# A graph layer's row gathers: each held for the one two ahead, and the whole ring filled early

## The reference: what is computed

```python
w_full = jnp.einsum('rb,bdo->rdo', w_comp, weight)      # 16 relations from 8 bases
x_rel = jnp.einsum('nd,rdo->rno', feat, w_full)
msg = x_rel[etypes, src] * norm                         # one message per edge
agg = jax.ops.segment_sum(msg, dst, num_segments=N)     # summed by target node
out = agg + h_bias + feat @ loop_weight                 # relu, added to x
...
gate_logits = x @ gate_w + gate_b                       # top 2 of 16 experts
h = relu(einsum('bsh,ehf->bsef', x, w1) + b1)
expert_out = einsum('bsef,efh->bseh', h, w2) + b2
```

## Time and profile before

| | us |
|---|---|
| median of three runs | 3274.21 |
| lowest and highest | 3268.51, 3275.11 |
| span of the profiled execution | 3302.6 |
| GpSimd busy in it | 1809.3 (55%) |
| tensor engine busy in it (matmul) | 2355.1 (71%) |
| DVE, ACT busy in it | 965.9, 658.4 |
| gathers of the layer (L1060), busy and idle before | 1463.5, 974.7 |

### The profile page before, as it was taken

How to read it: one execution, slowest core, us unless ns; L and a number is a source line. 1 busy time by engine, 2 the same in 40 slices (tenths; PEclk the granted TensorE clock), 3 DMA queues, 4 the chain that set the end, 5 groups by cost and what they waited for, 6 DMA issues and landing times. The chain is left out here.

```text
span 3302.6 us, 40335 instructions
## 1 busy us (share of the span) xinstructions
PE 2355.1 (71%) x11549; PEld 1953.5 (59%) x11550; DVE 965.9 (29%) x2172; ACT 658.4 (20%) x1539; POOL 1809.3 (55%) x2000
## 2 busy tenths in 40 slices
PE   2579898877778766767757565654744547999987
PEld 1467777666667555545545454543533337999986
DVE  6352332332223211222122121211211235333338
ACT  3232322222112211101110100000000004333336
POOL 0536566566565665656656566566565612555544
PEclk9699999888889888888878777876876678999999
DMA  6243333333333333323333332222322245122236
GB/s 214 85 133 97 108 96 105 94 97 116 96 97 95 107 96 93 96 87 94 106 90 90 93 95 88 86 85 83 91 85 82 81 127 211 70 70 70 69 95 229
DMA packets 146266, 338.62 MB, mean 103 GB/s; under 512 B 36674, under 2 KB 56290, under 8 KB 146051
## 3 DMA queue, kind: packets, MB, share of 16 engines
q0 software_dynamic: 89296, 245.33, 24.9%
q1 hardware_dynamic: 39311, 59.54, 5.2%
q10 hardware_dynamic: 17588, 32.88, 3.0%
HBM read 292.84 MB, written 47.97 MB: 103 GB/s over the span
## 5 line engine op out<-in xcount | busy, mean ns | idle before, releaser
L1060 POOL DMA_INDIRECT rows<-feat,idx x1540 | 1463.5, 950 | 974.7 <-DMA rows<-feat,idx 552.8
L1271 PE MATMUL psW<-rows,S 128*128 x3920 | 1155.5, 462 | 675.5 <-SPq L1016 647.9
L1271 PEld LDWEIGHTS psW<-rows,S 128*128 128x128 f32 x3920 | 910.0, 237 | 916.7 <-issue 752.3
L1142 DVE TENSOR_TENSOR S<-psHere,coefS 128x896 f32<-128x896 f32 x280 | 302.0, 1090 | 1798.9 <-PE psW L1271 1334.8
L1330 ACT COPY z<-psW 128x512 f32<-128x512 f32 x196 | 114.6, 585 | 1820.1 <-PE psW L1271 1185.2
L1236 PE MATMUL psG<-wb,zT 128*128 128x256 f32 (+1 forms) x1600 | 353.9, 379 | 0.5 <-issue 0.5
L1236 PEld LDWEIGHTS psG<-wb,zT 128*128 128x128 f32 (+1 forms) x1600 | 300.4, 188 | 46.5 <-issue 1.2
L1721 PE MATMUL psH<-xT,w1x 128*128 128x128 f32 x1840 | 227.0, 277 | 0.2
L1721 PEld LDWEIGHTS psH<-xT,w1x 128*128 128x128 f32 x1840 | 216.6, 193 | 2.0 <-issue 1.9
L1730 PE MATMUL psO<-w2s,hT 128*128 x912 | 215.7, 379 | 0.0
L1672 POOL DMA_INDIRECT expert_rows<-os,at_rows x114 | 113.1, 992 | 172.6 <-DVE os L1779 172.6
(11 more groups left out here) (284 smaller groups left out, 1472.2 us busy)
## 6 DMA issues: line engine op xcount, KB each, us to landing
rows<-feat,idx POOLq DMA_INDIRECT x1568
g<-expert_rows SPq DMA_DIRECT2D x24, 512.0 KB, 5.5
w1s<-in_L_ffn_w SPq DMA_DIRECT2D x8, 1024.0 KB, 10.0
w2s<-in_L_ffn_w SPq DMA_DIRECT2D x16, 512.0 KB, 9.9
feat<-rows SPq DMA_DIRECT2D x24, 256.0 KB, 3.0
fts<-feat ACTq DMA_DIRECT2D x24, 256.0 KB
h<-in_x ACTq DMA_DIRECT2D x24, 256.0 KB
y_rows<-y ACTq DMA_DIRECT2D x24, 256.0 KB
```

The costliest lines, as they stand in the source:

```text
L1060: e.indirect_dma_start(rows[:, at * H:(at + 1) * H], None, d.feat, bass.IndirectOffsetOnAxis(ap=idx[:, q * GB + u:q * GB + u + 1], axis=0) ...
L1142: e.tensor_tensor(S[h0 + h][:, :].rearrange("p (s b n) -> p s b n", s=U, b=B), both[:, h * U:(h + 1) * U, :].unsqueeze(2).to_broadcast([P, ...
L1271: last = e.matmul(psW[:, bass.ds(bank[u], H)], S[h][:, u * ZC:(u + 1) * ZC], rows[:, bass.ds(slot[u], H)], start=False, stop=True, skip_gr ...
```

## The change

GpSimd waits at every row gather, for the gather two ahead of it (`AHEAD` = 2), where before it waited at each seventh for the seven ahead. For this the eight semaphores are dealt out to the gathers in turn (`j % ROWS`), not by groups of seven slots, and SP counts each gather by itself. `EG` goes from 2 to 4, so 56 blocks, the whole ring, are gathered in `expand`, 4 behind each edge gather and 24 at the end. Registers that hold counts to wait for are now raised to at least one by an instruction of their own.

```diff
-QB = 7
+ROWS = 8
+AHEAD = 2
-EG = 2
+EG = 4
+def at_least_one(e, loaded, held):
+    for to, of in zip(held, loaded):
+        e.reg_alu(to, of, 1, ALU.max)
+    return held
...
             def ahead(j):
-                e.indirect_dma_start(rows[:, j * H:(j + 1) * H], ...).then_inc(s_row[j // QB], 16)
+                if j >= AHEAD:
+                    e.wait_ge(s_row[(j - AHEAD) % ROWS], 16 * ((j - AHEAD) // ROWS + 1))
+                e.indirect_dma_start(rows[:, j * H:(j + 1) * H], ...).then_inc(s_row[j % ROWS], 16)
...
             def rows_in(i):
-                for q in range(RB // QB):
-                    e.wait_ge(s_row[q], 16 * QB * (i + 1))
-                    e.sem_inc(s_in, QB)
+                for j in range(RB):
+                    e.wait_ge(s_row[j % ROWS], i * (RB // ROWS * 16) + (j // ROWS + 1) * 16)
+                    e.sem_inc(s_in, 1)
...
             def landed(i, n):
-                e.wait_ge(s_row[n % RB // QB], i * (IB * GB // RB * 16 * QB) + (n // RB + 1) * 16 * QB)
+                e.wait_ge(s_row[n % ROWS], i * (IB * GB // ROWS * 16) + (n // ROWS + 1) * 16)
                 e.sem_inc(s_paced, 1)
...
-                free = [e.snap(r, min_val=1, max_val=TURNS) for r in regs]
+                free = at_least_one(e, regs, room_held)
...
                     for u in range(GB):
                         at = (q * GB + u) % RB
-                        if u % QB == 0:
-                            landed(i, q * GB + u - QB)
-                        e.indirect_dma_start(rows[:, at * H:(at + 1) * H], ...).then_inc(s_row[at // QB], 16)
+                        landed(i, q * GB + u - AHEAD)
+                        e.indirect_dma_start(rows[:, at * H:(at + 1) * H], ...).then_inc(s_row[at % ROWS], 16)
...
-                        tile1 = e.snap(regs[AT_TILE], min_val=1, max_val=NT2)
                         with e.If(e.snap(regs[AT_ENDED], min_val=0, max_val=1)):
-                            tile_product(tile1, TW)
-                        clear = e.snap(regs[AT_CLEAR], min_val=1, max_val=NWP // 2)
-                        come = e.snap(regs[AT_COME], min_val=1, max_val=NBLK)
+                            tile_product(e.snap(at_least_one(e, regs[AT_TILE:AT_TILE + 1], tile_held)[0], min_val=1, max_val=NT2), TW)
+                        clear, come = at_least_one(e, [regs[AT_CLEAR], regs[AT_COME]], held)
```

More of the change, by code:

```diff
@@ L80 @@
 GB = 14
-QB = 7
+ROWS = 8
+AHEAD = 2
 IB = 2 * (RB // GB)
-EG = 2
+EG = 4
 CTL_PART = (84, 72, 64, 60)
-assert NBLK % RB == 0 and RB % GB == 0 and RB % QB == 0 and sum(CTL_PART) == TURNS and all(n % NS == 0 for n in CTL_PART)
+assert NBLK % RB == 0 and RB % GB == 0 and RB % ROWS == 0 and AHEAD < ROWS and sum(CTL_PART) == TURNS and all(n % NS == 0 for n in CTL_PART)
 assert all(t + n <= 8 * i <= TURNS for t, n, i in CHUNK)
@@ L711, in ahead @@
             def ahead(j):
-                e.indirect_dma_start(rows[:, j * H:(j + 1) * H], None, d.feat, bass.IndirectOffsetOnAxis(ap=idx[:, j:j + 1], axis=0)).then_inc(s_row[j // QB], 16)
+                if j >= AHEAD:
+                    e.wait_ge(s_row[(j - AHEAD) % ROWS], 16 * ((j - AHEAD) // ROWS + 1))
+                e.indirect_dma_start(rows[:, j * H:(j + 1) * H], None, d.feat, bass.IndirectOffsetOnAxis(ap=idx[:, j:j + 1], axis=0)).then_inc(s_row[j % ROWS], 16)
             for g in range(SG):
@@ L1030, in _ @@
             ch = Chain(e, s_pool)
-            regs = [e.alloc_register(f"room{q}") for q in range(IB)]
+            regs, room_held = ([e.alloc_register(f"{n}{q}") for q in range(IB)] for n in ("room", "room_held"))
             last = NBLK // (IB * GB) - 1
@@ L1057, in blocks @@
                         at = (q * GB + u) % RB
-                        if u % QB == 0:
-                            landed(i, q * GB + u - QB)
-                        e.indirect_dma_start(rows[:, at * H:(at + 1) * H], None, d.feat, bass.IndirectOffsetOnAxis(ap=idx[:, q * GB + u:q * GB + u + 1], axis=0)).then_inc(s_row[at // QB], 16)
+                        landed(i, q * GB + u - AHEAD)
+                        e.indirect_dma_start(rows[:, at * H:(at + 1) * H], None, d.feat, bass.IndirectOffsetOnAxis(ap=idx[:, q * GB + u:q * GB + u + 1], axis=0)).then_inc(s_row[at % ROWS], 16)
             e.iota(choice[1][:, :], [[1, X]], base=-X, channel_multiplier=0, allow_small_or_imprecise_dtypes=True).then_inc(s_xno, 1)
@@ L1118, in nodes @@
                 last.then_inc(s_y, 1)
-            regs = [e.alloc_register(f"look{k}") for k in range(2)]
+            regs, look_held = [e.alloc_register(f"look{k}") for k in range(2)], [e.alloc_register("look_held")]
             def look(i):
                 e.load(regs, pairs[0:1, bass.ds(i, 1), :])
-                tile1 = e.snap(regs[1], min_val=1, max_val=NT2)
                 with e.If(e.snap(regs[0], min_val=0, max_val=1)):
-                    nodes(tile1, P)
+                    nodes(e.snap(at_least_one(e, regs[1:2], look_held)[0], min_val=1, max_val=NT2), P)
             def pair(i, t0, c0, h0):
@@ L1254, in _ @@
             regs = [e.alloc_register(f"ps{u}") for u in range(CTL)]
+            held, tile_held = [e.alloc_register(f"ps_held{k}") for k in range(2)], [e.alloc_register("tile_held")]
             for part_of, n_turns in enumerate(CTL_PART):
@@ L1315, in _ @@
                 e.dma_start(to[0:1, :], zero[0:1, :]).then_inc(s_st, 16)
-            regs = [e.alloc_register(f"end{k}") for k in range(TW // 2)]
+            regs, ends = ([e.alloc_register(f"{n}{k}") for k in range(TW // 2)] for n in ("end", "end_held"))
             def tiles(t, nw):
                 e.load(regs, wend[0:1, bass.ds(t * (TW // 2), TW // 2)])
+                end = at_least_one(e, regs, ends)
                 base, groups = t * NE, HC * nw // 4
@@ L1327, in tiles @@
                         features_in(t, nw * WIN // 2)
-                    e.wait_ge(s_P, regs[k])
+                    e.wait_ge(s_P, end[k])
                     bank = psW[:, k % NB * BANK:(k % NB + 1) * BANK]
@@ L1750, in _ @@
         def _(e):
-            regs = [e.alloc_register(f"gx{k}") for k in range(SB + 2)]
+            regs, part_held = [e.alloc_register(f"gx{k}") for k in range(SB + 2)], e.alloc_register("part_held")
             e.wait_ge(s_bt, 1)
@@ L1761, in copy_w1 @@
             def copy_w1(k, ex):
-                e.wait_ge(s_wx, e.snap(ex // EG + 1, min_val=1, max_val=len(s_win)))
+                e.reg_alu(part_held, ex // EG + 1, 1, ALU.max)
+                e.wait_ge(s_wx, part_held)
                 e.tensor_copy(w1x[k][:, :], w1s[:, bass.ds(ex, 1), :, :].rearrange("p e c f -> p (e c f)")).then_inc(s_w1, 1)
@@ L2026, in program @@
                   [sb(f"choice{k}", [P, NT, X]) for k in range(K)], sb("both", [P, X, NT], BF16))
-        sent, got, s_row, s_xin, s_out, s_win = sems("sorted", 2), sems("got", 8), sems("row", RB // QB), sems("x_in", XS), sems("x_out", 2), sems("w_in", 4)
+        sent, got, s_row, s_xin, s_out, s_win = sems("sorted", 2), sems("got", 8), sems("row", ROWS), sems("x_in", XS), sems("x_out", 2), sems("w_in", 4)
         with nc.sbuf_tensor("ident_i", [P, P], F32) as ident_i:
```

## The result

| | before | after |
|---|---|---|
| median, us | 3272.49 | 3608.20 |
| lowest to highest | 3268.51 to 3275.11 | 3602.93 to 3610.14 |
| ratio, 95% interval | | 1.1024 (1.1008 to 1.1040) |
| span of the profiled execution | 3302.6 | 3608.2 |

The change costs 336 us, 10%. The prediction had the direction and the mechanism; its 3500 us is 108 us short, and its range ended at 3560.

The account below looks back on a forecast made before the run. GpSimd's gather pace was taken as the bound: first layer gather at 224 plus 1511 x 1.775 puts the last at 2906, +249 us on 3302.6, so 3552; weighing 3523 and 3453 two to one gave 3500 us, range 3425 to 3560.

Parts of the forecast that it names:

- What bounds the kernel: The layer's loop: GpSimd's own gather pace, 1.598 us each, sets the end; the tensor engine waits 636.6 us for rows.
- Start to start 3.55, two gathers in flight give 3.55 / 2: Layer gathers: each starts at least 3.55 us after the one two ahead, so 1.775 us each against 1.598.
- the pace term: Layer gathers after the change: 1.775 us each, kept within 1.73 to 1.82, over 1511 intervals.
- However the two are spaced ... the mean is the same: Layer gathers in pairs: spaced 1.25 and 2.30 us or evenly, the mean stays 1.775 us.
- The lead: Before the layer: 28 more gathers fill 34.10 idle us; layer opens at 200, first gather waits for third turn, about 224.
- Small things: SP's single counting, held registers and the stream's end: hidden by waits or unchanged; registers 28 us if that cover were gone.
- If the 28.4 lie anywhere but in the landings, they come off once: Profiled execution was 28.4 us above the median; subtracting that from 3552 gives 3523 us, weighed two to one.
- a reading of 3453: If the 28.4 us lie all in the 219 landing waits, pace is 1.71 and time 3453 us.
- A: Rival on layer gathers: landings come sooner with two in flight; at pace 1.525, some 3145 us; chance 0.05.
- B: Rival on layer gathers: landing shortens a little or the loss is partly hidden; pace 1.65, 3334 us; chance 0.04.
- D: Rival on layer gathers: the waits never bind and the lead alone counts; at pace 1.598, 3256 us; chance 0.01.
- C: Rival on layer gathers: loads and stores slow landings on every wait; pace 1.875, +400 us, 3674 us; chance 0.05.

Follow-up runs that it names:

- e6_ahead1: The changed kernel, but each gather waits for the one right ahead of it, so only one is in flight: 6313.5 us, one run.
- e3_wait: The changed kernel with 28 blocks gathered ahead instead of 56 (EG 2): 3634.4 us, 1.0981 of the kernel before.
- e7_after: The changed kernel unaltered, run again in another set: 3613.6 us, 1.0941 of the kernel before at 3305 us.
- e13_ahead3: The changed kernel with each gather waiting for the third last, so three in flight, a repeat: 3585 us, 1.0859 of the kernel before.

## Why the prediction was right in its direction and wrong in its size

- *What bounds the kernel* (GpSimd's pace): right. Every run that moved the pace without slow steps moved the time by it; 641 to 649 us follow the last gather in all of them.
- *Start to start 3.55, two gathers in flight give 3.55 / 2*: right as a mechanism. e6_ahead1 measures 3.553 with one in flight (middle value 3.518); after, the middle value over two gathers is 3.528. **But the mean is 3.626, and this is the first failed step: the pace term, taken at 1.775 (1.73 to 1.82), is 1.813.** 0.038 x 1511 = 57 us. The step that does not hold is "However the two are spaced ... the mean is the same": only the quiet round trip is halved, to 3.528 / 2 = 1.764, and what delays GpSimd beyond it counts in full. Above the quiet pace stand (1.813 - 1.764) x 1511 = 74 us, of two kinds.

  *Stops of GpSimd itself, 36 us.* At each 106th gather a wait passes and the gather behind it starts 3.33 us later instead of 0.75. First GpSimd's timeline at one such place, then the source view of the wait (L1050) from 1198 to 1202 us: the second wait passes at 1199.8.

```profile
1197.03 0.94 POOL L1069 DMA_INDIRECT rows<-feat,idx  x1 [0.43 <-issue]
1199.15 0.94 POOL L1069 DMA_INDIRECT rows<-feat,idx  x1 [1.18 <-DMA rows<-feat,idx]
1203.13 0.94 POOL L1069 DMA_INDIRECT rows<-feat,idx  x1 [3.03 <-issue]
1204.38 0.95 POOL L1069 DMA_INDIRECT rows<-feat,idx  x1 [0.30 <-issue]
```

```profile
L1050 POOLq EVENT_SEMAPHORE  x2: 17/17/17, 1198.4 to 1199.8; - x2
```

  There are 14, 2.58 us each, in after, and as many, as long and as far apart in gathers in e3_wait, e7_after and e6_ahead1. What GpSimd does then is open. In the kernel before a gather starts 0.9 us late at each 70th, 21 times, 19 us, within what the prediction called "loop heads and stretched issues"; for the changed kernel it has no such term.

  *Late landings, most of the other 38 us.* Of the waits without a list copy, 94 passed over 0.15 us above the middle value of 1.82, against 21 in e6_ahead1, 82 in e7_after and 99 in e3_wait. The prediction named late landings, had them in its mean of 2.50, and halved them with the rest. But GpSimd works in order, so the gather behind a late one is held too: seven late landings of after that stand alone and are over 0.5 us late come to 5.1 us, and moved the stream of gathers by 5.1, not by half (in e7_after 8.5 and 7.7). And they are more with two in flight, above all beside other transfers: where other DMA queues started over 16 KB from 0.5 us before to 1.8 us behind the end of the issue, 72 of 137 waits were late, elsewhere 22 of 1253; in e6_ahead1 11 of 61, and 10 of 1330.
- *The lead*: right. Opening 202.76 (200), first gather 225.3 (224), the third turn as the one waited for. That is the quicker kind of set; on the slower one e7_after has 214.31 and 236.4.
- *Small things*: right. Held registers nothing, in three runs; the tail 643.7 against 645.7.
- **The second failed step: "If the 28.4 lie anywhere but in the landings, they come off once", and the weighing with a reading of 3453.** Together they took 3552 down to 3500. The 28.4 us were a difference between sets of runs in the kernel before, and after hardly has it: 3608 and 3614 us. Nothing was to be taken off. 57 + 52 = 109 us, and 3500 + 109 = 3609.
- *The rivals*: A falls with e6_ahead1 (no shorter landing), B and D with the pace. C was nearer in size (1.813 lies between 1.775 and its 1.875), and partly right in cause: the middle landing did not slow, but its loads and stores "falling on every wait instead of one in seven" go with most of the late ones. That this traffic causes them was not tested by a run without it.
- *The range*: its high end took a pace of 1.80 on the reading of 3523. Even the 1.82 that the text gave as the term's bound ends at 3591 there; only with the 28.4 us left in does it hold 3608 (3552 + 0.045 x 1511 = 3620).

## What to carry to other kernels

A wait per item instead of per group divides the landing latency by what is in flight: two in flight cost half of it for each. Divide only the quiet latency; late landings and stops of the issuing engine count in full, since an engine that works in order holds back whatever stands behind. To hold a rate, space the work evenly; a wait on completion does it only at the price of the latency. And a difference between one profile and the runs' median may come from where the profile was taken: do not take it off a forecast before it is known that the changed kernel has it.

## What the runs showed of the hardware

- In three sets of five (before at 3305 to 3310 us), indirect gathers issued each 1.25 us for more than some 6 to 11 us made the small sequencer instructions of other engines take about 0.7 us instead of 0.02 to 0.06. The kernel went from the 2870 us that it takes elsewhere to 3585 and more. Half the bytes changed nothing (3640), 1.47 us between gathers removed it (3199). In two (before at 3271 and 3272) it did not occur, in whole rows or half. What differs, the chips or their condition then, is open; so is whether it explains before's own 1%: its loop has a few such steps on the slower kind, but it was not profiled on the other.
- With waits at every gather, GpSimd stopped for 2.58 us beyond the wait at each 106th gather, 14 times, in four runs of both kinds (after, e3_wait, e7_after, e6_ahead1).
- Of the landings with two in flight, 72 of 137 beside over 16 KB of other queues' transfers came over 0.15 us late, and 22 of 1253 without.
- On issue without a stop, the Trainium skill (DMA: Bandwidth & Descriptors, Anatomy of one DMA) says of descriptor generation: "You can emit a lot of descriptors before the incremental cost shows up". For GpSimd itself the trace agrees (0.95 us each as the middle value, at any rate). In e13_ahead3 a cost shows up on the other engines; that it is one of the descriptors no run isolates.
- A list copy of 0.20 us between two gathers costs 0.06 us, since 0.30 us of gap becomes 0.16 behind it; a clear of 0.35 us costs 0.22.
